# Between two decoder layers: a new order of combine, normalise and quantise for the first sequences, and clears moved on GpSimd

## What is computed

```python
x = x + _L0_attn_ref(_layernorm(x, axis=-1), ...)
x = x + _L0_xattn_ref(_layernorm(x, axis=-1), ctx_512, ctx_512, ...)
x = x + _L0_ffn_ref(_layernorm(x, axis=-1), ...)
x = x + _L1_attn_ref(_layernorm(x, axis=-1), ...)
x = x + _L1_xattn_ref(_layernorm(x, axis=-1), ctx_512, ctx_512, ...)
x = x + _L1_ffn_ref(_layernorm(x, axis=-1), ...)
```

## Time and profile before

| | us |
|---|---|
| median of 3 runs | 1855.13 |
| lowest, highest | 1852.25, 1860.34 |
| the profiled execution | 1852.35 |
| its span | 1850.7 |

### The profile page before, as it was taken

How to read it: one execution, slowest core, us unless ns; L and a number is a source line. 1 busy time by engine, 2 the same in 40 slices (tenths; PEclk the granted TensorE clock), 3 DMA queues, 4 the chain that set the end, 5 groups by cost and what they waited for, 6 DMA issues and landing times.

```text
span 1850.7 us, 24852 instructions
## 1 busy us (share of the span) xinstructions
PE 1370.4 (74%) x8316; PEld 984.7 (53%) x8316; DVE 1043.4 (56%) x2199; ACT 500.6 (27%) x1196; POOL 438.0 (24%) x519
## 2 busy tenths in 40 slices
PE   3676775666667599962659878599686797776988
PEld 1554554454464366641448755378453686544865
DVE  5355445436536233327766676666667665876654
ACT  2231222222223122211224312244113343132430
POOL 1141052134025200016422112221112321032210
PEclk8796687688679699985779979699897799997999
DMA  9300010065002311111200000000000000000000
GB/s 377 154 10 1 1 55 6 0 264 225 0 16 101 130 46 46 46 35 47 87 0 2 17 1 11 1 1 17 1 10 1 1 17 1 1 10 1 2 1 9
DMA packets 22248, 81.17 MB, mean 44 GB/s; under 512 B 3692, under 2 KB 7788, under 8 KB 20592
## 3 DMA queue, kind: packets, MB, share of 16 engines
q1 hardware_dynamic: 16496, 68.88, 9.9%
q0 software_dynamic: 5632, 10.77, 2.0%
HBM read 40.10 MB, written 39.52 MB: 43 GB/s over the span
## 4 chain that ended last, share of the span: by engine, by line
issue 44%; PE 29%; POOL 12%; DVE 9%; POOLq 2%; ACT 2%; DVEq 2%; DMA 1%; SPq 0%; ACTq 0%
PE ps L913 6%; PE ps L1133 4%; PE ps L932 3%; PE ps L1141 2%; POOL headbd L595 2%; PE ps L508 2%; POOL experts L1415 2%; POOL bd_hi L611 2%; PE ps L451 2%; POOL bd_lo L611 1%; PE ps L459 1%; POOL xn L494 1%; POOL small L408 1%; POOL tok_d L1387 1%; DVE x L1963 1%
## 5 line engine op out<-in xcount | busy, mean ns | idle before, releaser
L1318 ACT ACTIVATE probs<-ps,small 100x361 f32<-100x361 f32 x256 | 141.4, 558 | 194.9 <-DVE small L1924 194.9
L1924 DVE TENSOR_REDUCE small<-ps 100x2 f32<-100x722 f32 x128 | 116.0, 908 | 105.5 <-PE ps L960 105.5
L595 POOL TENSOR_TENSOR headbd<-kT,cst 128x800 f32<-128x800 f32 x64 | 97.4, 1525 | 194.8 <-DVE kT L1812 117.1
L433 PE MATMUL ps<-cst,xn 100*128 100x100 f32 x256 | 50.8, 351 | 121.4 <-DVE xn L397 83.6
L508 PE MATMUL ps<-headbd,qT 128*100 128x400 f32 x256 | 116.8, 539 | 20.0 <-POOL headbd L595 15.3
L913 PE MATMUL ps<-every,xT_t 128*128 x256 | 122.3, 601 | 0.4 <-issue 0.4
L1133 PE MATMUL ps<-hT,experts 128*128 128x400 f32 x288 | 117.8, 560 | 1.2 <-DVE small L628 1.2
L1084 PE MATMUL ps<-cst,probs 100*121 100x100 f32 x768 | 104.8, 273 | 12.4 <-ACT probs L1318 12.4
L958 PE MATMUL ps<-k_hi,bd_hi 128*100 128x362 f32 x256 | 103.6, 405 | 10.2 <-DVE bd_lo L611 10.2
L433 PEld LDWEIGHTS ps<-cst,xn 100*128 100x128 f32 x256 | 35.7, 197 | 138.6 <-DVE xn L397 85.2
L1084 PEld LDWEIGHTS ps<-cst,probs 100*121 100x121 f32 x768 | 97.3, 189 | 20.6 <-issue 7.8
(11 more groups left out here) (297 smaller groups left out, 2890.6 us busy)
## 6 DMA issues: line engine op xcount, KB each, us to landing
tok_d<-wt SPq DMA_DIRECT2D x1, 14848.0 KB, 45.8
res_d<-wt SPq DMA_DIRECT2D x1, 14848.0 KB, 48.9
every<-e_d SPq DMA_DIRECT2D x8, 1536.0 KB, 18.3
ctxT<-ctxT_d SPq DMA_DIRECT2D x8, 726.0 KB, 5.0
x_t<-tok_d POOLq DMA_DIRECT2D x32, 128.0 KB, 2.4
res_d<-out_t SPq DMA_DIRECT2D x32, 128.0 KB, 1.7
experts<-e_d SPq DMA_DIRECT2D x1, 3456.0 KB, 10.7
wt<-w_d SPq DMA_DIRECT2D x1, 3134.0 KB, 13.8
```

Of the source, the lines that this page charges most:

```text
L595: inc(e.tensor_tensor(headbd[:, u % 2], keysT[:, c, b * S:(b + 1) * S].unsqueeze(1).broadcast_to([P, HC, S]), cs("head").unsqueeze(2).broa ...
L1318: ins = e.activation(f_e[:, n % 2, i, 0:LC], bank(2 * (n % 2) + i, S, LC), ACT.Exp, bias=h_nm[:, n % 2, i:i + 1], accum_out=h_sum[:, b, h: ...
L1924: inc(e.tensor_reduce(h_nm[:, n % 2, 0:2], ps[0:S, 2 * (n % 2):2 * (n % 2) + 2, 0:LC], AX, ALU.max, negate=True), "F_nm")
```

## The change

- GpSimd, behind the token loads of the expert stage of layer 0: wait until the last tile's `hid_t` is transposed, clear y (100 x 1024), drain. This stands ahead of the wait for the last stores.
- GpSimd, behind the first 8 gathers: the norm of the first half comes at once, then the six clears of the value strips, then the norm of the second half. The 24 other gathers follow as before.
- VectorE: only pair 0 is combined ahead of the rounds. Then the first two steps of the first half (statistics; xn, gain and quantisation for the first projection), then pair 1, then the first step of the second half (statistics), then the rounds. The remaining pairs begin after three rounds that are left; against the steps of the halves that is one round later than before.

```diff
@@ -1406,6 +1406,9 @@
                 e.dma_start(x_t[:, t % NXT, :], tok_d[bass.ds(at, P), :]).then_inc(ld_xt[t % NXT].sem, 16)
+            e.wait_ge(t_hTp.sem, NTILE)
+            e.memset(y[:], 0.0)
+            e.drain()
             for i in range(NOT):
                 e.wait_ge(st_ot[i].sem, 16 * ((NTILE - 1 - i) // NOT + 1))
 
@@ -1417,8 +1420,7 @@
             for q in range(NB):
                 fetch(q)
-            for u in range(NVU):
-                e.memset(spread[:, u, :], 0.0)
+
             def before_e(g, h):
                 yield from norm_pool(e, "E_", g, h, eps2=EPS_RMS, fold=True)
 
@@ -1436,7 +1438,10 @@
-            in_turn(late(before_e(0, 1)), before_e(0, 0))
+            list(before_e(0, 0))
+            for u in range(NVU):
+                e.memset(spread[:, u, :], 0.0)
+            list(before_e(0, 1))
             for q in range(NB, NSEQ):
                 fetch(q)
             e.drain()
@@ -1767,7 +1772,7 @@
-            list(combine(range(HB)))
+            list(combine(range(1)))
             e.drain()
 
@@ -1899,7 +1904,13 @@
-            in_turn(late(before_e(0, 1)), before_e(0, 0), late(combine(range(HB, NSEQ // HB)), 4))
+            first_half, second_half = before_e(0, 0), before_e(0, 1)
+            next(first_half)
+            next(first_half)
+            list(combine(range(1, HB)))
+            e.drain()
+            next(second_half)
+            in_turn(second_half, first_half, late(combine(range(HB, NSEQ // HB)), 3))
```

## The result

| | before | after |
|---|---|---|
| median, us | 1854.61 (6 runs, 1852.25 to 1860.34) | 1873.28 (6 runs, 1870.96 to 1878.22) |
| the profiled execution | 1852.35 | 1871.69 |
| its span | 1850.7 | 1870.0 |
| granted TensorE clock | 0.839 | 0.834 |

The ratio is 1.0093, with a 95% interval of 1.0076 to 1.0110: slower, and outside the range of 1851 to 1862. The last store of layer 0 was issued at 819.96 before and at 822.4 after; before this point the two kernels do the same, and the same store came between 819.8 and 823.2 in all the traces of this study, variants that gained among them. So positions are compared from this store on ("+3.1" is 3.1 us later after the store than in the kernel before). The 19.3 us between the two spans are some 2.5 us ahead of it and 16.9 us behind it.

The account below looks back on a forecast made before the run. The prediction took GpSimd's start of the 24 gathers, 849.71, to bound the stretch. L408 at 834.7 plus a 15.28 us path put them at 850.0, 0.3 us later: 1855.13 + 0.3 = 1855.4 us, range 1851 to 1862.

Parts of the forecast that it names:

- Part 1: VectorE's new order of combine, normalise, quantise between the layers: alone, with today's 4.28 us drain, gathers start 2.9 us later.
- 15.28 us by the sum: Path over VectorE and GpSimd from L408's start to the 24 gathers: 15.28 us, against 7.08 before.
- Part 2: GpSimd's early clear of y and drain: hidden in idle time; L408 at 834.7, gathers at 850.0, 0.3 us later.
- R1: Rival: the drain's 4.28 us belong to its place, not to a count; +2.9 us, 1858.0 us, chance 0.25.
- unexplained 0.65 us: GpSimd drain ahead of L408: added to 1.01 us, from the last drain's 2.98 against 2.33 by count.
- Part 3: Six value-strip clears behind GpSimd's first 1/std: 5 us of cover, 2.87 us if uncovered; may hold up xn.
- R2: Rival: clears stop VectorE's xn, up to 1.7 or 2.87 us, taken as 1.1; +1.4, 1856.5 us, chance 0.10.
- 0.3 forecast: Start of the 24 gathers on GpSimd: 0.3 us later, giving a median of 1855.4 us, chance 0.50.
- Part 4: VectorE's tail: last combines end at 891.26, hidden by 0.67 us; TensorE's first transposes 8 us earlier, nobody held up.
- everything is rigid: Behind the start of the gathers: 24 gathers at their own pace, drain, headbd and scores follow that moment unchanged.

Follow-up runs that it names:

- b_drain_only: Kernel before plus only the clear of y and its drain on GpSimd: 1851.16 us, ratio 0.9979.
- b_stats_first: Kernel before plus early y clear and drain; first half's statistics ahead of pair 1, its quantising after pair 1 and second half's statistics: 1852.25 us, ratio 0.9982.
- a_no_y: Changed kernel without the clear of y and its drain: 1873.65 us, ratio 1.0102 to the kernel before.
- a_after: Changed kernel run once more without an edit, on chip 4: 1871.87 us, ratio 1.0074 to the kernel before.
- a_pool_only: Kernel before with only GpSimd's part of the change, VectorE as before: 1854.75 us, ratio 0.9997.
- c_after_late2: Changed kernel with the other pairs' combines one round earlier (late by 2, not 3), on chip 3: 1870.20 us, ratio 1.0058 to the kernel before.
- c_early4: Changed kernel with combines late by 2 and four of the 24 gathers put between the halves' norms: 1865.63 us, ratio 1.0036 to the kernel before.
- e_after_held: Changed kernel with TensorE's first transposes held until the second half is quantised, on chip 8: 1857.93 us, ratio 1.0022 to the kernel before.
- d_few_gathers: Kernel before with only VectorE's part of the change and only the last 4 of the 24 gathers, on chip 8: 1865.44 us, ratio 1.0053.
- b_late2: Kernel before with only VectorE's part, other pairs' combines one round earlier (late by 2, not 3), on chip 15: 1864.87 us, ratio 1.0055.
- a_vec_only: Kernel before with only VectorE's new order, GpSimd as before, on chip 4: 1874.84 us, ratio 1.0097.
- late 2: Other pairs' combines one round earlier than in the change (2, not 3); with the first half quantised ahead of pair 1, ratios 1.0055, 1.0058 and 1.0036.
- e_dummy_wait: Only VectorE's part, plus a TensorE wait on what its next instruction waits for anyway, on chip 8: 1860.74 us, ratio 1.0031 to the kernel before.

## Why the prediction was wrong, step by step

**Part 1** (the reorder costs 2.9 us on the way to the gathers) was right in its working. From L408 to the gathers it was 15.28 us by the sum and 855.30 - 837.79 = 17.51 in the trace. The 2.23 us between them are one row, xn at 3.21 us instead of 0.74 (+2.47), less 0.24 elsewhere.

**Part 2**: right in kind. The clear of 0.95 us and its drain were hidden, since the first gather still waited for the store, and the drain that cost 4.28 us costs 0.99 in b_drain_only and 1.06 in b_stats_first (L406 837.07, L408 838.13), when it has only 8 transfers behind it and they lie some microseconds back. It stands in the same place as before, so R1 is out. What I had put down as an unexplained 0.65 us for a drain right behind gathers measured 2.34 - 1.01 = 1.33 (L406 at 835.45, L408 at 837.79); a_no_y shows that it is no term to be added to any count. So L408 came 15.4 us after the store instead of 14.7.

**Part 3** and R2: the mis-sized term. I gave R2, the clears stop VectorE, one chance in ten and 1.1 us. It happened, wherever clears stand behind a 1/std, with 3.21 to 3.27 us each time (after, a_after, a_pool_only, a_no_y, c_after_late2, c_early4, e_after_held); without clears there it is 0.73 or 0.74. All instructions of L397 in this stretch of after, with min/median/max in ns:

```profile
L397 DVE TENSOR_SCALAR xn<-xall,small x4: 396/410/2898, 840.8 to 855.1; 100x256 f32<-100x256 f32 x4
```

One of the two instructions is held for 2.90 us, as long as all six clears (2.85), the other takes 0.40. My step was to price the wait at 0.84 us from another place, where the line was once held up; my own upper bound, "all six clears, 2.87", was the value. The Trainium skill (SBUF — State Buffer, Who interferes with whom) says that one waits for the whole instruction of the other; by this trace it is the whole row of clears, not one of them. In a_pool_only the same 2.5 us cost nothing: the drain gave them back (gathers at -0.7).

The three together: 0.3 forecast, +0.7 for the drain, +2.2 for the path, so 3.2 against 3.1 measured. And with TensorE on time the whole change then costs 3 to 4 us (e_after_held, on another chip). So the sum was off by 2.9 us for known reasons, in terms that the rivals had named.

**Part 4** is the step that failed. I wrote that TensorE's first transposes come 8 us earlier and "nobody is held up by them now", and that behind the gathers everything is rigid. The last eight combines were to be hidden up to 0.67 us of delay; in the trace VectorE was put back by three waits for TensorE and had 12 combines left at 895.60, so that the scores waited for it: +12.4 us at the first row maximum where I had +0.3. Set beside e_after_held, where TensorE was on time and the orders of VectorE and GpSimd are the same: the twelve combines begin 73.2 us after the store instead of 63.6, which is 9.6 us for the lateness, and they take 11.29 us instead of 9.41, another 1.9, since more of them now run beside GpSimd's headbd, as two did in the earlier trace rows. With the +1.7 that e_after_held has itself, this is the +13.2 at the last combine. (TensorE's first transposes came 4.8 us earlier against the store, at 848.01 and 850.35 in the two traces, not 8.) No row that I had read of the kernel before shows a group of TensorE whose signal comes 3 us after its work, so I couldn't have priced it; but I could have left room for it. The range was built from the forecast and its rivals, all on GpSimd's path, and its slower end was the scatter of a median. I had given 0.04 to a change for the worse that I had not seen. That the forecast of the path was near the measured +3.1 does not save it: the path to the gathers was not what held the kernel.

**Behind the stretch**, the last output is at +16.9 and the first row maximum at +12.4: another 4.5 us go after it. The granted clock shows 2.3 of them. TensorE had its first scores done at 901.0 and then stood idle for 8.86 us, up to 909.88, because VectorE was still combining. In this idle time the clock fell, and it stayed at 0.50 for 10 us over the next products and scores; in the kernel before it was 1.00 (2.4 GHz) from 893.6 on, 1.7 us into its first row maximum. First after, then before:

```profile
906.00:916.30 10.30, 6.42 (x30) 4.33 (x34) 7.02 (x11) 2.46 (x3) 1.43 (x1) 0.50 0.86 341
893.60:920.00 26.40, 20.85 (x194) 12.15 (x194) 22.01 (x30) 12.03 (x15) 9.19 (x8) 1.00 0.28 118
```

The fifth row maximum is 15.16 us behind the first in after (906.81 to 921.97) and 12.84 before (891.93 to 904.77). d_few_gathers, whose last twelve combines take 11.29 us too, has 0.50 from 899.0 to 909.3. The rest is open. b_late2 has +4.5 at its last combine and +17.1 at the last output without this low stretch (its profiled execution was its slowest of five), and the same quantities differ by some microseconds among kernels that end alike (a_after +20.3, after +16.9). No run changed the clock alone, so that the clock costs the 2.3 us is read from the rows, not shown by an experiment.

**What stays open** is why TensorE is late. Shown: it is in 8 traces of 20, always from the same group of TensorE on (the second half's second transposes; in four of the eight the group before it is 0.6 us late already) and over within 20 us. On one chip VectorE's new order brings it and GpSimd's part alone does not (a_vec_only against a_pool_only), and no trace without the first half quantised ahead of pair 1 has it. It is absent from the traces with one more wait or 18 more matmuls in TensorE's program, with 20 gathers fewer, and from one of three with late 2; but all of these are from chips 8 and 15, so a property of the chip is a rival that nothing here rules out. Against it speaks only that the kernel before takes nearly the same time on chips 4, 8 and 15 (1854.4 to 1855.1; 1858.5 on chip 3). The clock was 0.50 with the lateness and without it. One candidate is the supply of TensorE's instructions: an instruction transfer of 8 KB starts at 873.7 in after, inside the stretch. Against it: in e_dummy_wait, without late groups, the same transfer starts at 875.1, 1.0 us after the end of the same group, where it was 0.4 us in after; it takes 0.3 to 0.6 us in all the traces, and the trace doesn't say which engine it feeds. It wasn't tried further.

## What to carry to other kernels

- In this kernel a GpSimd drain took 0.08 us for each transfer that the engine had issued since its last drain; put one where the engine waits anyway. That alone was worth 3.5 us.
- Before moving a fill on GpSimd, look at what VectorE does at that moment: a tensor_scalar in SBUF waited for the whole run of six fills, a combine for none.
- An order on one engine can move another engine's work into a bad place that no sum of durations shows. When a change loses far more than its path explains, look at who waits for whom with nothing in between. A cure is no proof without its controls: a harmless edit in the same place, and the uncured kernel run again beside it, on the same chip.

## What the runs showed of the hardware

- Signals of TensorE came 3.4 to 7.3 us after the modelled end of their group, four groups in a row, and the idle times of those who waited repeated to 0.1 us in four traces of that order. In the traces with one more wait in its program, all from another chip, they did not; the cause is open.
- Six consecutive clears of 0.47 us on GpSimd held one VectorE tensor_scalar of 0.41 us for 2.90 us.
- The step with a GpSimd drain took 4.3 us after 48 transfers of its own (the last just issued or not), 1.0 us after 8, 0.68 after 4 and 0.34 after none, and 2.3 us with the last of 8 just issued.
- The granted clock was 0.50 over 10 us of first scores that followed 8.86 us in which TensorE stood idle, and 1.00 where it had no such gap.
